# Softmax sums in four 32-column tiles, inverses spread by DMA, and the scaling moved one phase later, in a fused two-layer transformer kernel

## The reference

```python
q = layernorm(xn @ Wq)                 # 16 heads of 64
k, v = split(xn @ Wkv)                 # 4 groups of 64; k is layer-normed
dots = einsum("bghqd,bgkd->bghqk", q, k) * 64 ** -0.5
attn = softmax(dots, axis=-1)          # over 1024 keys
out  = einsum("bghqk,bgkd->bghqd", attn, v)
x    = x + out @ Wout
```

## Time and profile before

| what | us |
|---|---|
| median of 3 runs | 820.09 (818.63 to 829.69) |
| the profiled execution, its own time | 818.38 |
| its span, first to last instruction | 816.6 |

### The profile page before, as it was taken

One profiled execution on the slowest core, in us unless ns is written; L12 is line 12 of the kernel. 1 busy time (PEld: TensorE's weight loads), 2 busy tenths in 40 slices (PEclk: granted clock), 3 DMA queues, 4 the chain that ended last, 5 costly groups with the idle time before them and its releaser, 6 DMA issues.

```text
span 816.6 us, 14237 instructions
## 1 busy us (share of the span) xinstructions
PE 789.5 (97%) x5002; PEld 473.0 (58%) x5002; DVE 631.7 (77%) x1147; ACT 525.0 (64%) x955; POOL 588.8 (72%) x385
## 2 busy tenths in 40 slices
PE   5998999999999999999899999999999999999998
PEld 4664455555555555567545555555555555987787
DVE  6997788888888787376877888887888876678774
ACT  3875566676667776668656766676777666555522
POOL 2777777888888888946567888788888796455840
PEclk9999999999999999999999999999999999999999
DMA  6000000000000000000000000000000002200001
GB/s 184 1 2 1 0 2 2 1 1 1 1 1 2 1 2 1 1 0 2 1 1 2 1 1 1 2 1 2 1 1 1 2 1 53 56 1 2 1 1 53
DMA packets 49745, 8.03 MB, mean 10 GB/s; under 512 B 42502, under 2 KB 48266, under 8 KB 49674
## 3 DMA queue, kind: packets, MB, share of 16 engines
q1 hardware_dynamic: 48810, 6.99, 5.4%
q10 hardware_dynamic: 864, 0.13, 0.1%
HBM read 5.92 MB, written 1.05 MB: 9 GB/s over the span
## 4 chain that ended last, share of the span: by engine, by line
PE 89%; DVE 6%; ACT 2%; issue 1%; DMA 1%; POOL 0%; SPq 0%; DVEq 0%; POOLq 0%; ACTq 0%
PE psum L724 29%; PE psum L709 22%; PE psum L689 11%; PE psum L739 4%; PE psum L1850 4%; PE psum L752 3%; DVE part L1280 2%; PE psum L1861 2%; PE psum L575 2%; PE psum L1888 2%; PE psum L577 1%; PE psum L576 1%; PE psum L1918 1%; PE psum L1836 1%; PE psum L668 1%
## 5 line engine op out<-in xcount | busy, mean ns | idle before, releaser
L544 POOL TENSOR_TENSOR space<-space 128x1024 f32<-128x1024 f32 x160 | 381.7, 2385 | 23.7 <-ACT space L973 5.9
L973 ACT ACTIVATE space<-psum 128x512 f32<-128x512 f32 x512 | 264.1, 605 | 37.2 <-PE psum L709 36.3
L724 PE MATMUL psum<-space,vb 128*64 128x512 f32 x1024 | 247.5, 605 | 2.1 <-ACT space L973 2.1
L1280 DVE TENSOR_REDUCE part<-psum 128x2 f32<-128x1024 f32 x150 | 183.1, 1221 | 31.5 <-PE psum L689 31.4
L724 PEld LDWEIGHTS psum<-space,vb 128*64 128x64 f32 x1024 | 62.5, 136 | 120.4 <-issue 61.4
L549 POOL TENSOR_TENSOR space<-space 128x1024 f32<-128x1024 f32 x30 | 71.7, 2392 | 77.9 <-DVE space L1298 77.9
L689 PE MATMUL psum<-kh,qh 64*128 64x512 f32 x512 | 119.0, 453 | 4.7 <-DVE part L1280 4.7
L1276 DVE TENSOR_REDUCE part<-psum 128x1 f32<-128x512 f32 x106 | 73.2, 690 | 52.2 <-PE psum L689 52.2
L709 PE MATMUL psum<-qh,kh 64*128 64x512 f32 x512 | 105.7, 395 | 0.0
L689 PEld LDWEIGHTS psum<-kh,qh 64*128 64x128 f32 x512 | 49.9, 183 | 95.6 <-DVE part L1280 59.3
L709 PE MATMUL psum<-qh,kl 64*128 64x512 f32 x512 | 105.2, 389 | 0.0
(11 more groups left out here) (252 smaller groups left out, 1131.9 us busy)
## 6 DMA issues: line engine op xcount, KB each, us to landing
ql<-nmx SPq DMA_DIRECT2D x256, 0.5 KB, 2.0
wproj<-in_L_ffn_W SPq DMA_DIRECT2D x4, 256.0 KB, 3.7
out<-x SPq DMA_DIRECT2D x3, 256.0 KB, 2.0
x<-in_L_attn_x SPq DMA_DIRECT2D x2, 256.0 KB, 4.5
wproj<-in_L_attn_Wq SPq DMA_DIRECT2D x1, 512.0 KB, 6.6
x<-in_L_attn_x SPq DMA_DIRECT2D x1, 512.0 KB, 7.5
wout<-in_L_attn_Wout SPq DMA_DIRECT2D x1, 512.0 KB, 6.8
w1s<-in_L_ffn_W SPq DMA_DIRECT2D x2, 256.0 KB, 2.7
```

The lines of the kernel that those rows point to most:

```text
L544: pool.tensor_tensor(to, pt[0] if u == 1 else to, pt[u], ALU.add)\
L724: last = pe.matmul(outp[rows(h), :], vb[:, place(m)[1], kt, :], pt[kt][:, h, :], start=(kt == 0), stop=(kt == TILES - 1))
L973: act.activation(pt[kt][:, h, :], key_scores[kt % 2][h], ACT.Exp).then_inc(exp_made, 1)
L1280: dve.tensor_reduce(to[:, half, :], scores.rearrange("p (h k) -> p h k", h=2), AX_X, ALU.max, negate=True)\
```

## The change

All slots but the last of each batch are *brief* (`is_brief`), 30 of 32. For these:

- `add_up` makes four matmuls in place of two. Each multiplies 256 columns of `acc` (one `h`, one `hp`) by ones of 32 columns and writes 32 partitions of `sums`, so that the sums of the four heads lie in four blocks of 32 equal rows and 256 columns.
- Logarithm, guess and Newton step work on 128 by 256 elements in place of 128 by 512. The step's two instructions stand together at the end of `k = 1` (`correct_brief`), and write `brief`.
- SyncE waits for the second of them (`fix_made`) and issues four DMAs (`spread_rinv`). Each copies one row of 256 values of `brief` to 64 partitions of `rinv`. They are for the slot two before the one whose maxima SyncE is at, and stand ahead of the wait for that slot's last pair. For the last brief slot of a batch they stand after all the maxima.
- `scale` waits for the four DMAs (`rinv_spread`), reads `rinv` in place of the sums' place in PSUM, and stands in the middle of `k = 3`.

```diff
+        guess_at = vecs[:, :, :].rearrange("p k d -> p (k d)")
+        brief = cross[:, :, :].rearrange("p k d -> p (k d)")
...
+        def is_brief(n):
+
+            return n % SLOTS < SLOTS - 1
+
+        def brief_rows(h, hp):
+
+            first = P // 4 * (PAIRS * h + hp)
+            return slice(first, first + P // 4)
...
+        def spread_rinv(sp, n):
+
+            sp.wait_ge(fix_made, 2 * n + 2)
+            for h in range(2):
+                for hp in range(PAIRS):
+                    one = brief_rows(h, hp).start
+                    sp.dma_start(rinv[rows(h), hp * QB:(hp + 1) * QB], brief[one:one + 1, :].unsqueeze(1).broadcast_to([1, DH, QB])).then_inc(rinv_spread, 16)
...
                     for pair in range(4):
                         t, hp = divmod(pair, PAIRS)
+                        if pair == 3 and m >= 2:
+                            spread_rinv(sp, n - 2)
                         sp.wait_ge(max_made, 4 * n + pair + 1)
...
+                spread_rinv(sp, SLOTS * b + SLOTS - 2)
...
-                terms = [acc[n % 2]]
-                if n % SLOTS == SLOTS - 1:
-                    terms = [pt[TILES - 2], pt[TILES - 1], acc[n % 2]]
+                if is_brief(n):
+                    pe.wait_ge(pool_added, ADDS * (n + 1))
+                    for h in range(2):
+                        for hp in range(PAIRS):
+                            last = pe.matmul(sums[brief_rows(h, hp), 0:QB], c["ones_square"][:, 0:P // 4], acc[n % 2][:, h, hp * QB:(hp + 1) * QB],
+                                             start=True, stop=True)
+                    last.then_inc(sums_made, 1)
+                    return
+                terms = [pt[TILES - 2], pt[TILES - 1], acc[n % 2]]
...
+            def correct_brief(n):
+
+                at = sums[:, 0:QB]
+                dve.wait_ge(rinv_made, n + 1)
+                dve.tensor_tensor(at, at, guess_at, ALU.mult).then_inc(fix_made, 1)
+                dve.wait_ge(fix_made, 2 * n + 1)
+                dve.scalar_tensor_tensor(out=brief, in0=at, scalar=2.0, in1=guess_at, op0=ALU.subtract, op1=ALU.mult).then_inc(fix_made, 1)
...
-                dve.wait_ge(fix_made, 2 * n + 2)
                 dve.wait_ge(out_kept, n + 1)
-                dve.tensor_tensor(ot, ot, sums_of(n), ALU.mult).then_inc(ot_made, 1)
+                if is_brief(n):
+                    dve.wait_ge(rinv_spread, spread_count(n))
+                    dve.tensor_tensor(ot, ot, rinv, ALU.mult).then_inc(ot_made, 1)
...
-                    if k == 2 and 0 <= m < SLOTS:
+                    if k == 2 and m == SLOTS - 1:
                         correct(n, 1)
...
+                    if k == 3 and 0 <= m < SLOTS - 1:
+                        scale(n)
                     if mine_at < SLOTS:
                         largest(SLOTS * b + mine_at, 2 * mine_k + 1)
-                    if k == 1 and 0 <= m < SLOTS:
+                    if k == 1 and 0 <= m < SLOTS - 1:
+                        correct_brief(n)
```

More of the change, by code:

```diff
@@ L301, in first_layer @@
         rinv_made = sem("rinv_made")
+        rinv_spread = sem("rinv_spread")
         fix_made = sem("fix_made")
@@ L369, in rows, with spread_count @@
             return slice(h * DH, (h + 1) * DH)
+        def is_brief(n):
[3 more added lines that the diff above has]
+            return slice(first, first + P // 4)
+        def spread_count(n):
+            return 16 * 4 * (n - n // SLOTS + 1)
         def place(m):
@@ L998, in take_log @@
                     act.wait_ge(ot_made, n)
-                act.activation(rinv, sums_of(n), ACT.Ln).then_inc(log_made, 1)
+                if is_brief(n):
+                    act.activation(guess_at, sums[:, 0:QB], ACT.Ln).then_inc(log_made, 1)
+                else:
+                    act.activation(rinv, sums_of(n), ACT.Ln).then_inc(log_made, 1)
             def invert(n):
                 act.wait_ge(log_made, n + 1)
-                act.activation(rinv, rinv, ACT.Exp, scale=-1.0).then_inc(rinv_made, 1)
+                at = guess_at if is_brief(n) else rinv
+                act.activation(at, at, ACT.Exp, scale=-1.0).then_inc(rinv_made, 1)
             def produce(b):
@@ L1368, in scale @@
             def scale(n):
-                dve.wait_ge(fix_made, 2 * n + 2)
                 dve.wait_ge(out_kept, n + 1)
-                dve.tensor_tensor(ot, ot, sums_of(n), ALU.mult).then_inc(ot_made, 1)
+                if is_brief(n):
+                    dve.wait_ge(rinv_spread, spread_count(n))
+                    dve.tensor_tensor(ot, ot, rinv, ALU.mult).then_inc(ot_made, 1)
+                else:
+                    dve.wait_ge(fix_made, 2 * n + 2)
+                    dve.tensor_tensor(ot, ot, sums_of(n), ALU.mult).then_inc(ot_made, 1)
             def add(n):
@@ L1416, in attention @@
                         add_tail(n + 1, 1)
+                    if k == 3 and 0 <= m < SLOTS - 1:
+                        scale(n)
                     if mine_at < SLOTS:
                         largest(SLOTS * b + mine_at, 2 * mine_k + 1)
-                    if k == 1 and 0 <= m < SLOTS:
+                    if k == 1 and 0 <= m < SLOTS - 1:
+                        correct_brief(n)
+                    if k == 1 and m == SLOTS - 1:
                         correct(n, 0)
-                    if k == 2 and 0 <= m < SLOTS:
+                    if k == 2 and m == SLOTS - 1:
                         scale(n)
```

## The result

The changed kernel takes 1061.46 us (1059.86 to 1062.39), against 819.38 us for the kernel before in the same job: a ratio of 1.295, with a 95% interval of 1.291 to 1.298. Its profiled execution has a span of 1060.4 us, 243.8 more than before. The prediction was 1000, range 822 to 1080.

A forecast was written before the change was run, and what follows sets the result against it. TensorE was taken to bound the kernel, its waits paid in full slot by slot. Profiled 818.4 us, less 8.4 for the sums, plus 190 for the maxima's waits, gave 1000 us, range 822 to 1080.

The forecast's parts named there:

- The bound: TensorE bounds the attention's slots, busy 789.5 of 816.6 us; whatever makes it wait is paid in full, slot by slot.
- The sums: In add_up, four 256-column matmuls side by side cost 0.58 us, a gain of 0.28 over 30 brief slots: -8.4 us.
- rival 3: On TensorE, the four sum tiles run two at a time or singly, +4.5 or +30 us; chance 0.05 by itself.
- The maxima behind the spreads: First tile_scores of a slot waits 6.8 us for maxima DMAs queued behind the spreads, 28 times: +190 us.
- the Newton step and SyncE's start: On VectorE, the second Newton instruction ends at 150.07 and SyncE goes on at 150.10; last maximum there at 149.20.
- The data time of 8.3 us: Four spreads' data from one row each, the third beside the second: three times 2.75, 8.3 us, between 5.5 and 11.0.
- The estimate that the prediction works out from the Trainium skill: By DMA ports of about 27 GB/s, four spreads take 9.6 us one after another, 4.8 with ports side by side.
- An issue of 0.49: On SyncE, loads issued one behind the other start 0.49 us apart; taken for the four spreads' issues.
- Rival 1: One row reads as fast as many; only SyncE's issues count: 31 us wait, 841 us (827 to 858); chance 0.24.
- Rival 4: TensorE's clock falls to half speed in the long waits, 1.7 us less work 28 times: 1048 us; chance 0.05.
- 2.6 twice: Last brief slot of each batch has its spread exposed: 9.9 us where 7.3 lie before the projection, left to the range.
- What I cost at nothing: Halved logarithm, inverse and Newton step, and scale from two SBUF operands (0.81 for 0.69 us): no cost in the chain.

The follow-up runs named there:

- the 32-row kernel: The changed kernel, with each spread reading 32 equal rows of brief twice in place of one row 64 times: 868.68 us, ratio 1.060.

## Why the prediction was right, and where it was off

**The bound.** It holds: what TensorE waits for in a slot is paid in full, slot by slot.

**The sums.** The predicted 0.58 on the chain is 0.57, the predicted 0.28 a slot is 0.30. Four tiles do run side by side; rival 3 is out.

**The maxima behind the spreads.** The step that I took as the likeliest happened: 28 waits of 6.2 us, against 6.8, and 173 us against 190. Of its parts, the Newton step and SyncE's start are as worked out (the first spread is issued 0.83 us after the last maximum, 199.17 to 200.00, for 0.90). The data time of 8.3 us, chosen between 5.5 and 11.0, is 8.1 by the chain: the last maxima DMA lands at 210.00, 10.0 us after the first spread's issue, and 1.1, 0.2 and 0.6 of that were worked out for the start, the maxima's own pieces and the landing. The estimate that the prediction works out from the Trainium skill had 9.6 or 4.8 for it, to either side. That 8.3 and 8.1 agree is in part luck, for the pattern behind the 8.3 isn't there. The four spreads of this slot, from issue to landing:

```profile
DMA to landing us min/median/max: 4.6/6.1/7.8
```

The first lands at 204.6 and the last, issued at 201.84, at 209.6. The first takes 4.6 - 1.1 - 0.6 = 2.9 us of data, but the other three take 5.0 together, 1.7 each, where I had two of them side by side and each of these steps at 2.75. Of the 0.6 us between 6.8 and 6.2, 0.2 are this landing (10.0 for 10.2), and 0.4 come from TensorE, which is ready 3.8 us after the first spread's issue (210.05 less 6.20) for 3.4.

**An issue of 0.49.** This term was wrong: undisturbed spreads are issued 0.64 apart (200.56 to 201.20), and the last spread's issue takes 1.58 and the next 2.05 us, while the first spreads' data is still on its way. It cost little on top, since the data was the later of the two.

**Rival 1.** Its price, issues alone, is what the 32-row kernel shows: 1.6 us a slot for the predicted 1.1. It lost because one row isn't read as fast as many.

**Rival 4, the clock.** I had it as a rival with a chance of 0.05 and 48 us. It is not a rival but a part of the same case: some 55 us, 42 of them given back by keeping TensorE at work. A wait of 6 us on the engine that bounds the kernel should have brought its price along. With it the forecast would have been 1048; from there to 1061 are -17 for the wait, 7 more for the clock, 7 for the first `tile_scores` behind it, and 17 at the ends of the batches, of which I had named 5 (2.6 twice) and left them to the range. I had not named what stands behind the last spreads in SyncE's list, the next layer's weights.

**What I cost at nothing.** The scaling of two SBUF operands was taken as 0.81 in place of 0.69, from the row of `add_tail`. That row was a mean over two kinds: in the kernel before these additions mostly run while GpSimd waits, at 0.69, and a few take up to 2.9. In the changed kernel the error does not show, since GpSimd idles through the long waits, and the scaling at 209.74 takes 0.69 (once, at a batch's end, it takes 1.84). But it decides whether the change can be mended: with the DMAs gone, the kernel is 2.3% slower than before with it (839.5) and 1% faster without (812.0).

## What to carry to other kernels

A DMA that copies one SBUF row many times is held up by that one source; if the same values lie in more rows, reading those costs a third of the time (2.1 us to landing for 5.8). Before an operand moves from PSUM to SBUF, look at what GpSimd does at that moment, and look at minimum, median and maximum of such an instruction, not at the mean. And price a wait on the bounding engine with what the clock takes behind it.

## What the runs showed that I had not expected

- A VectorE instruction with two SBUF operands, 0.68 us alone, takes 2.2 us in the median beside a GpSimd that adds without a break, and the same instruction with one operand in PSUM (400 to 417 ns for 256 columns, sixty times) is not held up at all.
- SyncE's issue of a DMA, 0.5 to 0.6 us in most cases, grows to as much as 2.6 us for a spread and 2.3 for a maxima DMA while one source row is being read; no run shows what ties the two. With sources of 32 rows in the same order the longest are 1.1 and 1.4.
- After a wait of 6.25 us the granted clock was 0.55 over the next 7 us, and 0.77 after the next wait, of 6.20; with matmuls put into the waits it stayed at 1.00 in all but two of 28 slots.
